# Cross-attention with routed experts on one core: the order of the first loads, GpSimd splitting one expert, and statistics ahead of the low halves

## The reference, cut to what matters

```python
kp = ctx @ Wk.T;  vp = ctx @ Wv.T + bv;  qp = layernorm(x) @ Wq.T + bq
probs = softmax(qp @ kp.T / sqrt(512))
x = x + (probs @ vp) @ Wo.T + bo
xf = layernorm(x)
idx = argmax(softmax(xf @ Wg + bg))              # one expert of 8 for each row
h = gelu(xf @ W1[idx] + b1[idx])                 # W1, W2: 8 x 512 x 512
x = x + h @ W2[idx] + b2[idx]
```

## Time and profile before

| what | us |
|---|---|
| median of the runs | 456.88 |
| lowest and highest run | 456.77, 457.61 |
| the profiled execution | 461.18 |
| its span in the trace | 459.5 |
| preparation, up to the first transposes of x tile 0 | 113.76 |

### The profile page before, as it was taken

The page is one execution under the profiler, slowest core; times in us unless marked ns, Lnnn a source line. Parts: engine busy times, 40 slices in busy tenths (PEclk is TensorE's granted clock), DMA queues, the critical chain, the costliest instruction groups (busy, mean ns, idle before and its releaser), DMA issues.

```text
span 459.5 us, 7892 instructions
## 1 busy us (share of the span) xinstructions
PE 414.3 (90%) x2083; PEld 222.8 (48%) x2084; DVE 249.5 (54%) x615; ACT 211.6 (46%) x427; POOL 183.1 (40%) x233
## 2 busy tenths in 40 slices
PE   6968999998898998898898999899999999998990
PEld 2455665565766665665343334344444444443440
DVE  0255999777366766886456234444444454454430
ACT  1233346745787878786542563333333433332310
POOL 8000000600115444357264227556565655666421
PEclk9959999999999999999898999999999999999997
DMA  8999986840835547543797969798989999999620
GB/s 251 352 327 385 376 314 229 301 157 3 295 92 176 175 166 256 182 163 138 177 179 215 195 147 144 179 208 175 203 187 197 209 175 220 178 214 186 127 59 0
DMA packets 116006, 90.87 MB, mean 198 GB/s; under 512 B 86642, under 2 KB 86654, under 8 KB 115975
## 3 DMA queue, kind: packets, MB, share of 16 engines
q1 hardware_dynamic: 108735, 70.55, 60.3%
q0 software_dynamic: 6400, 19.65, 13.9%
q10 hardware_dynamic: 840, 0.29, 0.4%
HBM read 50.37 MB, written 21.06 MB: 155 GB/s over the span
## 4 chain that ended last, share of the span: by engine, by line
PE 65%; DMA 13%; DVE 5%; issue 5%; SPq 4%; ACT 4%; POOLq 0%; another core or an unknown queue 0%; DVEq 0%; POOL 0%; ACTq 0%
PE bank L1441 22%; PE bank L1444 11%; DMA work<-in_ctx 5%; PE bank L1354 5%; PE bank L1304 4%; PE bank L1374 4%; DMA expert_weights<-key_bias_then_xn 4%; PE bank L1392 4%; PE bank L1282 3%; DMA ey_bias_split_then_geluT<-work 3%; PE bank L1367 3%; DMA out_x<-keys_values_then_rows_b 2%; PE bank L1264 2%; PE bank L1432 1%; PE bank L1249 1%
## 5 line engine op out<-in xcount | busy, mean ns | idle before, releaser
L1441 PE MATMUL bank<-expert_weights 128*128 x312 | 76.6, 390 | 7.9 <-DMA expert_weights<-key_bias_then_xn 5.9
L653 POOL DMA_INDIRECT out_x<-keys_values_then_rows_b x39 | 44.3, 1135 | 82.2 <-DVE keys_values_then_rows_b L1141 71.6
L1441 PE MATMUL bank<-expert_weights,ey_bias_split_then_geluT 128*128 x312 | 73.8, 379 | 2.8 <-DMA ey_bias_split_then_geluT<-work 2.0
L833 ACT ACTIVATE work<-work 128x512 f32<-128x512 f32 x31 | 19.5, 630 | 107.0 <-DVE work L1195 107.0
L1141 DVE SCALAR_TENSOR_TENSOR keys_values_then_rows_b<-bank,keys_values_then_rows_b 128x512 f32<-128x512 f32 x39 | 27.0, 691 | 69.6 <-PE bank L1444 69.5
L1441 PEld LDWEIGHTS bank<-expert_weights 128*128 128x128 f16 x312 | 30.5, 99 | 47.4 <-issue 16.0
L709 ACT ACTIVATE expert_weights<-expert_weights 128x512 f16<-128x512 f32 x64 | 38.8, 626 | 29.2 <-DVE expert_weights L931 28.8
L1441 PEld LDWEIGHTS bank<-expert_weights,ey_bias_split_then_geluT 128*128 128x128 f16 x312 | 29.8, 98 | 41.1 <-issue 9.0
L613 POOL DMA_INDIRECT routed_rows<-work,slot_index x32 | 32.7, 1020 | 36.9 <-DVE slot_index L1025 29.4
L931 DVE SCALAR_TENSOR_TENSOR expert_weights<-expert_weights 128x512 f16<-128x512 f32 x64 | 41.5, 685 | 1.1 <-ACT expert_weights L709 0.6
L1444 PE MATMUL bank<-expert_weights 128*128 x156 | 40.7, 384 | 0.0
(11 more groups left out here) (186 smaller groups left out, 654.8 us busy)
## 6 DMA issues: line engine op xcount, KB each, us to landing
expert_weights<-in_L_ffn_W SPq DMA_DIRECT2D x14, 1024.0 KB, 9.8
keys_values_then_rows_b<-routed_rows SPq DMA_DIRECT2D x39, 258.0 KB, 3.1
expert_weights<-in_x SPq DMA_DIRECT2D x16, 512.0 KB, 9.0
expert_weights<-in_x SPq DMA_DIRECT2D x24, 256.0 KB, 3.3
routed_rows<-keys_values_then_rows_b POOLq DMA_DIRECT2D x9, 258.0 KB, 9.3
keys_values_then_rows_b<-in_x SPq DMA_DIRECT2D x8, 256.0 KB, 4.9
expert_weights<-in_L_ffn_W SPq DMA_DIRECT2D x8, 256.0 KB, 3.6
work<-in_ctx SPq DMA_DIRECT2D x1, 1920.0 KB, 21.1
```

Source lines behind the costliest of these rows:

```text
L653: pool.indirect_dma_start(out_rows, ids_of, rrow[t.buf][:, 0:D], None, bounds_check=T - 1, oob_is_err=False).then_inc(out_sent[t.buf], 16)
L1441: mm(o, a[:, c, :], w_split[:, bass.ds(first + (2 * c + h) * D, D)], start=(c == 0 and h == 0 and not begun), stop=False)
```

## The change

- **Loads.** After Wk and Wq come Wo, then `ctx` in two halves, then Wv, and only then the x groups 0 to 3. TensorE transposes Wo before `ctx`. The transposed Wo now lies in the area of the values, since both `ctx` and it would want the same place. The load of expert 5 moves behind those of x tiles 0 to 3.
- **Expert 0** is split by GpSimd alone (`POOL_UNITS`, `split`): three instructions of 128x512 for each of its eight units. ScalarE's and VectorE's counts skip these units (`shared`, `split_by`), and the ScalarE work on experts moves back by one expert.
- **VectorE** takes all sixteen groups of x with nothing but the low halves of J_OV between them. The low halves of experts 1 and 2 follow in one row, and with each J_VAL job come three low halves instead of two.
- **ScalarE** has no high halves among the J_OV copies, two with each J_KEYS copy (now experts 1 and 2), and normalises tile 0 before expert 5's high halves instead of after them.
- **Padding rows** are written after the scales of x, and VectorE waits for them ahead of the last J_VAL copy instead of the first. Two small loads (the broadcasts of bo and bg) are issued by ScalarE after the `ctx` copies.

```diff
-            load_group(0)
-            sp.dma_start(ctx_nat[0:K, :, :], ctx_in.rearrange("b k d -> k b d")).then_inc(ld["ctx"], 16)
-            load_group(1)
             sp.dma_start(wo_sb, chunked(Wo)).then_inc(ld["wo"], 16)
-            load_group(2)
+            for h in range(2):
+                sp.dma_start(ctx_nat[0:K, 4 * h:4 * h + 4, :],
+                             ctx_in[4 * h:4 * h + 4].rearrange("b k d -> k b d")).then_inc(ctx_half[h], 16)
             sp.dma_start(wv_sb, chunked(Wv)).then_inc(ld["wv"], 16)
-            load_group(3)
+            for n in range(NM):
+                load_group(n)
...
-            for e in range(E + 1):
-                pool.dma_start(routed[SPAN * e:SPAN * e + P, :], pad_row).then_inc(pad_out, 16)
+            def split(n):
+
+                pool.wait_ge(w_early[n // NW], 32)
+                if n >= GAP:
+                    split_by(pool, n - GAP)
+                src = wall[:, (n + GAP) * D:(n + GAP + 1) * D]
+                hi, lo = (w_split[:, n * 2 * D + D * h:n * 2 * D + D * (h + 1)] for h in range(2))
+                link(nc.gpsimd.tensor_scalar(src, src, WSCALE, 1.0, ALU.mult, ALU.mult))
+                link(nc.gpsimd.tensor_scalar(hi, src, 1.0, 0.0, ALU.mult, ALU.add))
+                nc.gpsimd.tensor_tensor(lo, src, hi, ALU.subtract).then_inc(pool_split, 1)
+
+            for n in POOL_UNITS:
+                split(n)
...
-                need(act, low_done, n - GAP + 1)
+                if n >= GAP:
+                    split_by(act, n - GAP)
...
             act.wait_ge(scal1, 3)
+            step(-1, U - 1, -1)
+            high_of(NEARLY - 1)
             act.wait_ge(pre_mm, NJOBS)
-            for k in range(-1, NT):
+            for k in range(0, NT):
...
+            for n in range(NW, 3 * NW):
+                low(n)
+                if n == NW + 9:
+                    dve.wait_ge(rows_split, 1)
...
-            dve.wait_ge(pad_out, 16 * (E + 1))
             for b in range(B):
                 n = J_VAL + b
                 ready(n)
+                if b == B - 1:
+                    dve.wait_ge(pad_out, 16 * (E + 1))
...
-                for m in range(2):
-                    low((NEARLY - 2) * NW + 2 * b + m)
+                for m in range(3):
+                    low((NEARLY - 3) * NW + 3 * b + m)
```

More of the change, by code:

```diff
@@ L271, in build @@
         bank = [ctx.enter_context(nc.psum_tensor(f"bank{n}", [P, D], F32)) for n in range(8)]
-        ld = {n: sem(f"loaded_{n}") for n in ("ctx", "wv", "wo", "wg", "bias", "bo", "bg")}
+        ld = {n: sem(f"loaded_{n}") for n in ("wv", "wo", "wg", "bias", "bo", "bg")}
+        ctx_half = [sem(f"ctx_half_{h}_loaded") for h in range(2)]
         wkq_in = [sem(f"wk_wq_chunk_{c}_loaded") for c in range(C)]
@@ L586, in _ @@
             nc.gpsimd.tensor_tensor(std1[:, :], ve1[:, :], rstd1[:, :], ALU.mult).then_inc(scal1, 1)
+            for e in range(E + 1):
+                pool.dma_start(routed[SPAN * e:SPAN * e + P, :], pad_row).then_inc(pad_out, 16)
             pool.wait_ge(pre_mm, NJOBS)
@@ L714, in _ @@
                 copy(n, kq[:, 0, k, :], bank[n % 8][:, :], WSCALE)
+            for k in range(C):
+                n = J_WOT + k
+                copy(n, woT[:, k, :], bank[n % 8][:, :])
             for b in range(B):
@@ L730, in _ @@
                     copy(n, wo_gate[:, :, :], bank[n % 8][:, 0:C * EM].rearrange("p (c e) -> p c e", c=C))
-                for m in range(2):
-                    high(2 * k + m)
-            act.wait_ge(w_early[1], 32)
-            for n in range(NW, 2 * NW):
-                high(n)
             for m in range(2 * C):
@@ L757, in _, with high_of @@
             nc.scalar.activation(bias_split[:, 0, :], key_bias[0:1, :], ACT.Copy).then_inc(bias_parts, 1)
-            for e in range(NEARLY - 2, NEARLY):
+            def high_of(e):
                 act.wait_ge(w_early[e], 32)
@@ L1242, in _ @@
             last.then_inc(pre_mm, 1)
-            pe.wait_ge(ld["ctx"], 16)
-            for b in range(B):
-                n = J_CTX + b
-                free(n)
-                for c in range(C):
-                    last = nc.tensor.transpose(bank[n % 8][:, K * c:K * (c + 1)], ctx_nat[0:K, b, P * c:P * (c + 1)],
-                                               ident[0:K, 0:K])
-                last.then_inc(pre_mm, 1)
             pe.wait_ge(ld["wo"], 16)
@@ L1259, in _ @@
                                                ident[:, :])
+                last.then_inc(pre_mm, 1)
+            for b in range(B):
+                n = J_CTX + b
+                free(n)
+                if b % 4 == 0:
+                    pe.wait_ge(ctx_half[b // 4], 16)
+                for c in range(C):
+                    last = nc.tensor.transpose(bank[n % 8][:, K * c:K * (c + 1)], ctx_nat[0:K, b, P * c:P * (c + 1)],
+                                               ident[0:K, 0:K])
                 last.then_inc(pre_mm, 1)
```

67 lines of the change are left out of this document (30 added, 37 removed).

## The result

The changed kernel took 456.26 us in the median of 22 runs (450.67 to 461.22), the kernel before 459.83 us in 22 runs on the same chips (456.06 to 464.04). The ratio of the two, with disturbed runs left out, is 0.9897, with a 95% interval of 0.9868 to 0.9926: faster by 1.0%, 4.7 us of 459.83, and between 3.4 and 6.1. I had forecast 449.5 us (447.5 to 453.6), a gain of 7.4. The direction was right. About a third of the forecast gain did not come, and the base was too low: the three runs shown beforehand had a median of 456.88, and all 22 runs of the same kernel, with those three among them, have 459.83. So of the 6.8 us between forecast and result, 3.0 are the base and 3.8 are gain that the medians of all runs do not show (they lie 3.6 apart; the ratio gives 4.7).

The account below looks back on a forecast made before the run. The preparation was taken as bound by the load of `ctx`, then by TensorE's own work. Gain 8.1 - 0.4 - 0.3 = 7.4 us, so 456.88 - 7.4 = 449.5 us, range 447.5 to 453.6.

Parts of the forecast that it names:

- The loads of `ctx`: Start of the preparation: even at the slow 218 GB/s, Wo and `ctx` land by 23 us, so TensorE has no load wait.
- J_OV 8.1 us earlier: J_OV starts at about 28.7 instead of 36.83 us: 5.5 us of idle time and 2.6 of clock saved.
- From J_OV to J_VAL TensorE's work is unchanged: Main stretch of the preparation: 36.83 to 91.78 us becomes 28.7 to 83.7, if nobody is late.
- Statistics end at 67: VectorE's statistics of x end at 67 us instead of 81.3; up to 69 us J_KB would not wait.
- rival 1: Statistics of x become the bound: ending at 70.4 to 73.1, they delay J_KB by 1.4 to 4.1 us; chance 0.13.
- GpSimd's splits: GpSimd splits expert 0 from about 32 us at 3.0 us a unit, 24 in all, done at 56 with 16 us slack.
- Rival 2: GpSimd's units delay the row weights and J_KB; the gain is used up at 5.65 us a unit; chance 0.06.
- The handover: From J_VAL to the first transposes of x: 0.4 us charged for the last copy, 0.3 us for the transposes' copy.
- From there the loop runs as before: After the copy of the first transposes of x: the loop is unchanged, so the stretch to the end stays 345.7 us.
- rival 3: GpSimd's scales and VectorE's low halves exclude each other, so J_KB comes 3.9 us late, for 453.4 us; chance 0.03.
- rival 4: Gain absent or given back by `ctx` loading or by loop and experts: 0 to 3 us stay, 453.9 to 457; chance 0.08.
- The signs of being wrong: Gap before J_KB over 1 us, a GpSimd unit over 4.6 us, or first transposes to end not 345.7 us within 1.

Follow-up runs that it names:

- cuts: Kernels ended after the first transposes of x and one store, without loop, routing and experts: kernel before 126.65 us, changed kernel 120.28 us.
- filled cut: The changed kernel's cut with throwaway products filling TensorE's idle time ahead of J_OV: 117.27 us, against 120.28 without them.
- x groups first: Changed kernel with x groups 12 to 15 loaded ahead of expert 2: 452.37 us, ratio 0.9828; the same edit in its cut: 117.56 us.
- changed again: The changed kernel unchanged, run again for a second trace: 456.75 us, ratio 0.9897 against the kernel before.
- filled: Full changed kernel with two throwaway float32 products in the 1.74 us idle time ahead of J_OV: 453.78 us, ratio 0.9887.
- the cut with the loads alone: Cut of the kernel before with only SyncE's load order changed (ctx whole, Wo, Wv, then x groups 0 to 3): 125.49 us.
- padding rows early: Cut of the changed kernel with the padding rows written right after GpSimd's constants, as before: 120.52 us, against 120.28.

## Why the prediction was right or wrong

The forecast failed in two terms: the base, worth 3.0 us, and the clock behind the waits that the new order keeps, which the sum put at nothing. The steps one by one:

- **What bounds the kernel: right.** The load of `ctx`, then TensorE. Everything that the change gained lies before J_OV: 8.6 us there in the first trace, 7.4 at the first transposes.
- **The loads of `ctx`: right by the slow end.** No wait ahead of Wo or `ctx` in any trace of the changed order with late padding rows. The rate between 12 and 22 us was the low one that I took from the earlier trace rows; the stretch in the changed kernel:

```profile
12.00:22.00 10.00, 10.00 (x36) 5.15 (x35) 3.04 (x6) 2.42 (x5) 0.00 (x0) 1.00 1.06 227
```

- **J_OV 8.1 us earlier: 8.6 in the first trace** (28.25), some 0.5 of it since the first products ended sooner. The idle time ahead of it was 1.74 us where I had 1.1.
- **"From J_OV to J_VAL TensorE's work is unchanged": the step that failed.** I counted the regained clock, 2.6 us, as a gain for good, and charged the idle stretch ahead of J_OV, which I had found myself, with its 1.1 us of length alone, and nothing for the clock behind it. In three traces of six the clock fell there, and J_OV took 25.2, 25.2 and 23.5 us instead of 21.8: 1.4 us on average over the six. Filling the stretch gave 2.6 to 3.0 us in the cuts; why more than 1.4 is open. The average is of six traces only, and in the trace of the filled cut the wait at J_KB was shorter too, 0.69 us. The clock that the change wins back at the `ctx` transposes is lost again half the time at J_OV, where the work is longer.
- **Statistics end at 67: 70.4** in the first trace, and 73.5 and 75.1 in executions with the slow J_OV (rival 1, at its mild end). The mis-sized term is the load of group 12, wanted at 58 and landed at 64: I had it land at 60.5 to 61. Expert 2 was issued at 52.3, as forecast (52.7), but not moved at 386 GB/s from there on: 50 to 56 us moved 66, 152 and 187 GB/s (rows above), and only from 56 on was the rate back at 335 and more. The row from the statistics to the row weights took 78.25 - 70.43 = 7.8 us, 8.5 forecast. The wait at J_KB was 1.27, 1.86 and 1.88 us in the traces of the changed kernel and its cut, and 0.24 where TensorE was late itself; behind the 1.86 the clock was low, and the products took 1.7 us longer. With the x groups first the cut gains 2.3 to 2.7 us.
- **GpSimd's splits: overpriced, with room.** One unit takes 2.53 us (3.0 forecast, and a little under the bound of 2.6), all eight are done at 57.8 (56). They began 5.6 us later than I had it, at 37.57, as expert 0 landed late. ScalarE waited for units 6 and 7 at 55.4 and 57.9 and nobody waited for that. Rival 2 was far off.
- **The handover: nearly right.** With three low halves for each J_VAL job VectorE kept pace: its last copy began at 105.57, 0.1 us after TensorE's end, so the 0.4 us that I charged did not come. The copy of the first transposes began 107.42 - 105.57 = 1.85 us later, 1.95 forecast. "From there the loop runs as before" was not quite so. The transposes of tile 1 now wait 1.77 us, where they waited 1.39. Before and after:

```profile
115.78 0.66 PE L1367 MATMUL bank<-identity,work 128*128 128x128 f32 x4 [1.39 <-ACT work L769]
108.76 0.66 PE L1387 MATMUL bank<-identity,work 128*128 128x128 f32 x4 [1.77 <-ACT work L794]
```

  Behind the longer wait the clock fell to 0.5 for 3 to 4 us in three of the six full traces of the changed kernel and its variants (changed again, x groups first, filled), and in neither of the two of before. From the first to the fifth tile's transposes it is 9.04 us in both traces of before, 9.42 or 9.43 where the clock stayed full, and 10.37, 10.62 and 10.77 where it fell. The cuts end ahead of this. In the changed kernel's second trace (columns as in the stretches of 48 to 58 us above):

```profile
110.00:112.00 2.00, 0.23 (x2) 1.00 0.17 49
112.00:114.00 2.00, 2.00 (x11) 0.53 0.88 323
114.00:116.00 2.00, 2.00 (x13) 0.61 0.97 302
```

- **The rule on the shared port pair (rival 3): not seen here.** GpSimd's 5.78 us operation ran from 71.28 to 77.06, and VectorE's low halves beside it at the usual pace:

```profile
73.41 1.29 DVE L955 SCALAR_TENSOR_TENSOR expert_weights<-expert_weights 128x512 f16<-128x512 f32 x2 [0.28 <-ACT expert_weights L735]
74.91 1.29 DVE L955 SCALAR_TENSOR_TENSOR expert_weights<-expert_weights 128x512 f16<-128x512 f32 x2 [0.20 <-ACT expert_weights L735]
```

  The Trainium skill (SBUF — State Buffer, section "Who interferes with whom") calls the shared port pair an exclusive lock, for which such a pair of operations contends. No operation of VectorE was held for the length of GpSimd's in these traces.
- **The rest of the kernel gives nothing back (rival 4): a little, at tile 1; beyond that open.** The preparation gained 6.4 us by the cuts, the whole 4.7 (3.4 to 6.1). The first transposes come at 115.0 on average in the three traces of before and its cut, and at 109.5 in the four of the changed kernel and its cut: 5.5 us, of which 0.4 go at the later copy. The fall of the clock at tile 1 costs another 0.9 to 1.4 us in half of the traces. From the first transposes to the end the traces took 345.7 and 345.4 us before and 344.3 and 345.3 after, which shows no loss; but other variants range from 341.8 to 351.1, with stretches of low clock at different places in each, and a difference of 1 to 2 us in the mean can't be told from that.
- **The range** failed on two counts: it took three runs of one chip as the kernel's level, and it had no term for the clock, whose cost changes from execution to execution. With the right base alone it would have held: moved up by 3.0 us it reaches 456.6, and the result is 456.26. The 0.2% that I took a measurement to tell was also too fine; 22 runs of before spread over 1.7%. And its lower end was a slip: 9.2 less the 0.3 of the handover gives 448.0, not 447.5.
- **The signs of being wrong.** Two of the three came already in the first trace: the gap before J_KB was 1.27 us, over 1, and the stretch from the first transposes to the end 344.3, 1.4 from the 345.7. No unit of GpSimd took over 4.6 us.
- **Luck.** That the first trace showed its first transposes exactly 7.4 us earlier bore out nothing. It is one of the executions in which the clock stayed full in the preparation; the second came at 109.44.

## What to carry to other kernels

An idle stretch of TensorE is not priced by its length alone: with the low clock behind it, 1.7 us of waiting cost up to 5 us here, so a gap of 1.4 to 2 us inside long busy work is worth a trial of closing or filling it. When a change moves work forward, look for the small waits that it leaves in the new order, and charge them a share of the clock. A base from three runs deserves its own term in the range, above all when a further execution already lies elsewhere, as the profiled one here did, 0.9% above the median of the three.

## What the runs showed of the hardware that I had not expected

- TensorE's granted clock fell to half for 3 to 7 us of wholly busy work after idle stretches of 1.74 us (ahead of J_OV, 3 of 6 traces), 1.77 us (tile 1, 3 of 6), 1.86 and 1.41 us (J_KB, in two cuts) and 1.48 us (J_KEYS, in the cut with the loads alone). It stayed full after others of 1.83 us (the second half of `ctx`, padding rows early) and 1.88 us (J_KB). Filling the first with products that are thrown away made the cut 2.6 to 3.0 us shorter in the median.
- While `ctx` landed, in 120 partitions, the loads moved at 227 GB/s (12 to 22 us) at a DMA share of 1.06; the stretches of loads into 128 partitions around it moved at up to 364 before it and 381 after. Why is open.
- The same kernel's preparation varied by 3.1 us between two traces through the landing of one transfer, 27.37 and 30.49 us, though nothing ahead of it had changed.
